# Pacing of interleaved work in a fused attention and FFN layer on eight cores

## What is computed

```python
def exterior(p1, p2):            # 6 components of p1 ^ p2, normalised
    parts = [p1[..., i] * p2[..., j] - p1[..., j] * p2[..., i] for i, j in _PAIRS]
    L = jnp.stack(parts, axis=-1)
    return L / jnp.maximum(jnp.linalg.norm(L, axis=-1, keepdims=True), 1e-12)

# attention: 16 heads, 6-component queries and keys, 64-wide values, causal
L_q = exterior((x @ W1_q.T).reshape(B, T, H, 4), (x @ W2_q.T).reshape(B, T, H, 4))
L_k = exterior((x @ W1_k.T).reshape(B, T, H, 4), (x @ W2_k.T).reshape(B, T, H, 4))
scores = jnp.einsum('bqhc,bkhc->bhqk', L_q, L_k @ _J6.T) * _SCALE
attn = jax.nn.softmax(jnp.where(causal, scores, -jnp.inf), axis=-1)
out = jnp.einsum('bhqk,bkhd->bqhd', attn, v) @ W_out.T + b_out
# FFN: W_real, W_imag are 512 x 512 each, unfolded from two small tensors
out_real = x_real @ W_real.T - x_imag @ W_imag.T + bias_real
out_imag = x_real @ W_imag.T + x_imag @ W_real.T + bias_imag
# layer: x + attention(xn) + ffn(xn)
```

## Time and profile before

| | us |
|---|---|
| median of 2 runs | 4972.77 (4968.52 and 4977.02) |
| the profiled execution | 4981.22 |
| its span, first to last instruction, slowest core (core 1) | 4980.2 |
| spans of all eight cores | 4961.6 to 4980.2 |
| busy: PE / DVE / ACT | 3447.8 / 1556.4 / 1477.3 |
| mean granted TensorE clock, cores 0 to 3 / 4 to 7 (median core) | 0.642 / 0.648 |

### The profile page before, as it was taken

The page is one execution under the profiler, slowest core; times in us unless marked ns, Lnnn a source line. Parts: engine busy times, 40 slices in busy tenths (PEclk is TensorE's granted clock), DMA queues, the critical chain, the costliest instruction groups (busy, mean ns, idle before and its releaser), DMA issues.

```text
span 4980.2 us, 37630 instructions; the slowest of 8 cores (4961.6 to 4980.2 us)
## 1 busy us (share of the span) xinstructions
PE 3447.8 (69%) x11040; PEld 1078.4 (22%) x11040; DVE 1556.4 (31%) x3089; ACT 1477.3 (30%) x1729; POOL 130.9 (3%) x197
## 2 busy tenths in 40 slices
PE   1137666777766866677766876677776787777776
PEld 0113211221111521222111432222111241111112
DVE  0543344432222334433122325533122222212211
ACT  0000033334422113333523203333433203454440
POOL 3000000000000000000000010000000000000001
PEclk9977855675555865576555775577555675555557
DMA  7100311120000131121000041112000021000004
GB/s 77 51 22 1 112 45 31 49 75 27 1 0 0 19 62 30 41 69 51 0 0 0 1 68 34 34 60 71 0 0 0 1 44 25 1 0 0 0 1 68
DMA packets 78284, 146.27 MB, mean 29 GB/s; under 512 B 39680, under 2 KB 42888, under 8 KB 78096
## 3 DMA queue, kind: packets, MB, share of 16 engines
q0 software_dynamic: 56000, 73.28, 7.8%
q1 hardware_dynamic: 22096, 70.59, 5.1%
HBM read 80.80 MB, written 69.21 MB: 30 GB/s over the span
## 4 chain that ended last, share of the span: by engine, by line
PE 53%; DVE 18%; DMA 10%; ACT 9%; issue 8%; DVEq 1%; POOL 0%; ACTq 0%; SPq 0%; POOLq 0%
PE O L546 16%; PE F L573 9%; PE S L506 8%; DMA y<-ost 7%; PE F L383 5%; DVE cdiv L579 3%; PE F L416 3%; DVE oT L587 3%; ACT exps L529 3%; ACT cdiv L566 2%; DMA xst<-x 2%; ACT cdiv L564 2%; PE F L423 2%; PE F L309 2%; DVE xnst L282 2%
## 5 line engine op out<-in xcount | busy, mean ns | idle before, releaser
L529 ACT ACTIVATE exps<-S 128x1024 bf16<-128x1024 f32 (+3 forms) x1280 | 1122.6, 893 | 2216.1 <-PE O L546 1559.1
L546 PE MATMUL O<-exps,vaug 128*65 128x512 bf16 (+3 forms) x2560 | 1075.4, 523 | 450.8 <-DVE oT L587 247.8
L506 PE MATMUL S<-fqp,fkp 6*128 6x512 bf16 x2560 | 709.2, 562 | 30.6 <-ACT exps L529 23.8
L573 PE MATMUL F<-cdiv,ones64f 1*64 1x512 f32 x512 | 461.0, 1051 | 206.1 <-ACT cdiv L566 201.0
L546 PEld LDWEIGHTS O<-exps,vaug 128*65 128x65 bf16 x2560 | 229.7, 138 | 982.9 <-issue 981.5
L579 DVE COPY cdiv<-F 64x512 f32<-64x512 f32 x256 | 164.0, 678 | 836.7 <-PE F L573 836.7
L537 DVE TENSOR_TENSOR exps<-exps,tri 128x256 bf16<-128x256 bf16 x512 | 142.7, 290 | 839.3 <-ACT exps L529 838.5
L295 PE MATMUL F<-idt,xnst 128*128 128x128 f32 x512 | 124.2, 424 | 351.9 <-DVE xnst L282 315.2
L506 PEld LDWEIGHTS S<-fqp,fkp 6*128 6x128 bf16 x2560 | 137.4, 98 | 881.4 <-issue 876.2
L456 PE MATMUL S<-wout,oT 128*128 128x512 bf16 x1024 | 271.3, 430 | 68.9 <-DVE ost L465 65.8
L383 PE MATMUL F<-wv,xnT 128*128 128x256 bf16 x2048 | 261.8, 291 | 3.3 <-DVE cdiv L579 3.1
(11 more groups left out here) (76 smaller groups left out, 2097.2 us busy)
## 6 DMA issues: line engine op xcount, KB each, us to landing
y<-ost POOLq DMA_DIRECT2D x128, 512.0 KB, 5.2
xst<-x SPq DMA_DIRECT2D x64, 512.0 KB, 3.6
xnst<-x SPq DMA_DIRECT2D x64, 512.0 KB, 4.3
wv<-wvT POOLq DMA_DIRECT2D x8, 256.0 KB, 18.1
wout<-woutT POOLq DMA_DIRECT2D x8, 256.0 KB, 18.6
tascr<-qk SPq DMA_DIRECT2D x16, 128.0 KB, 1.7
ost<-bout SPq DMA_DIRECT2D x1, 512.0 KB
ost<-bri SPq DMA_DIRECT2D x1, 512.0 KB
```

The source lines that it names most:

```text
L506: tS.inc(TE.matmul(S_ps[:, ss * 1024 + j * 512: ss * 1024 + j * 512 + 512], fk_pad[32 * m4:32 * m4 + 6, kt * 128:kt * 128 + 128], fq_pad[3 ...
L529: sS.inc(SE.activation(e_out, e_in, AF.Exp))
L546: ins = TE.matmul(O4[:, j * 512 + off:(j + 1) * 512], vaug[:, kt * 1040 + h * 65: kt * 1040 + h * 65 + 65], exp_sb[:, ss * 1024 + j * 512 ...
L573: tS.inc(TE.matmul(Fb[0:64, 0:512], ones64f_sb[:], cdiv[0:1, j * 512:j * 512 + 512], start=True, stop=True))
```

## The change

pace() no longer works at every fifth step but at every step, against a target that grows evenly over the 320 steps. The total is the sum of all weights, plus 4 for the V groups that are appended later. An item of weight 0 (A1) is charged 0.5 when it is taken, though it counts 0 in the total.

```diff
-            state = {"step": 0, "gate": False}
+            state = {"step": 0, "gate": False, "popped": 0.0}
+            total_items = sum(w for w, _ in q1) + sum(w for w, _ in q2) + (4 if b + 1 < nb else 0)
             def pace():
                 state["step"] += 1
-                if state["step"] % 5 == 0:
-                    wsum = 0
-                    while wsum < 1:
-                        if q1:
-                            w_, fn = q1.popleft()
-                        elif state["gate"] and q2:
-                            w_, fn = q2.popleft()
-                        else:
-                            break
-                        fn()
-                        wsum += w_
+                target = state["step"] * total_items / 320.0
+                while state["popped"] < target:
+                    if q1:
+                        w_, fn = q1.popleft()
+                    elif state["gate"] and q2:
+                        w_, fn = q2.popleft()
+                    else:
+                        break
+                    fn()
+                    state["popped"] += max(w_, 0.5)
```

## The result

The changed kernel takes 4949.94 us (median of 11 runs, 4942.92 to 4964.99) against 4981.15 before (10 runs): ratio 0.993, 95% interval 0.9911 to 0.995. When the forecast was made the kernel before had been timed only twice (4972.77).

What follows compares the result with a forecast made beforehand. The end is set by a chain of waits hopping between PE, ACT and DVE. Terms -5 + 16 + 9 + 2 = +22, taken as +20 a batch, +60 over three, gave 5041 profiled, 5033 us against the median; range 4975 to 5075.

Steps and rivals of the forecast that it cites:

- What bounds the kernel: Whole kernel: no engine full, a chain hops between PE, ACT and DVE; interleaved work adds to the path.
- Where the items go: In pace(): first queue ends at step 261, before 160; only 8 B items in the loop, the rest behind it.
- The tail and V: Behind the loop: last O to next first O grows from 122.2 to about 218 us; V itself +2 a batch.
- A: Normalising and transposing x tiles, split in two: sixteen tiles cost 84 us against 89.3, -5 us a batch.
- F: FFN passes, spread and moved: six at 6.9 us, ten at 3.0, 71 against 55, +16 us a batch.
- B in the loop: Eight B items in the loop cost 83 us; with four behind it 135 against 126.0, +9 us a batch.
- the signs that the prediction named: Changed profile: first to last O about 965 us, tail about 218, less transpose idle, FFN stage clock above 0.50.
- Rival 1: Interleaved items cost the same wherever they stand, only the order changes: 4973 to 4985 us; chance 0.14.
- Rival 2: First half of each A tile hides everywhere, three steps before the second: 4835 us, 2.8% faster; chance 0.04.
- Rival 3: FFN stage: clock stays at 0.50 through spread passes, 135 us a batch, 5225 us; chance 0.06, weaker forms included.
- Rival 4: Behind the loop: dense V groups are throttled, 9 us a batch more, 5060 us; chance 0.06.

Runs made afterwards that it cites:

- experiment 5: Changed kernel with only A's steps moved, first halves to 8, 19, 29, 36 of forty, second halves to 12, 24, 32, 40: 4796.9 us, ratio 0.9643.
- experiment 1: Changed kernel with B and V items put back at the steps of the kernel before: 4940.1 us, ratio 0.9907 to the kernel before.
- experiment 2: Changed kernel with A tiles and FFN passes put back at the steps of the kernel before: 4999.0 us, ratio 1.0038 to the kernel before.
- experiment 3: Changed kernel with the two halves of each A tile issued together again, at the second half's step: 5016.9 us, ratio 1.0074.
- experiment 6: Kernel of experiment 5 with the sixteen FFN passes of a batch all moved to ends of head pairs: 4709.9 us, ratio 0.9463.
- experiment 7: Changed kernel with DVE's square (L264) done twice: 5007.0 us, ratio 1.0055.
- experiment 8: Kernel of experiment 5 with all twelve B items in the loop and FFN passes at pair ends and unmasked steps: 4688.0 us, ratio 0.9418.
- experiment 9: Kernel of experiment 8 with four FFN passes and two B items moved to other steps: 4661.9 us, ratio 0.9358.
- experiment 4: Kernel before with only A split, first half three steps ahead of the second: 4985.3 us, ratio 1.001.

## Why the prediction was wrong, point by point

**What bounds the kernel.** Right for the places of both kernels: interleaved items are added to the path and not hidden, and each has a price of its place. It is no property of the items: at the places of experiment 5 sixteen tiles of A cost 12 to 18 us. Sums made in this way came within 1 to 8 us a batch in experiments 1, 2, 3, 5, 6, 7, 8 and 9; the one for experiment 4 (the split alone) missed by 19.

**Where the items go.** Right, by the windows.

**The tail and V.** Right: 95.7 us more were forecast behind the loop, 95 to 97 came. Experiment 2 isolates this half of the change and finds it a loss, as forecast.

**A, the step that failed first.** The forecast changed A by -5 us a batch, to 84, from four tiles at 20.9 us: 5.9, 8.0, 5.0 and 2.0. (Three slips of the working change nothing: 7.3 - 1.5 - 0.3 is 5.5 and not 5.6, the upper bound of F is 134 and not 135, and the window of 20.1 us holds steps 91 to 95 and not 90 to 95.) Steps 41 to 81 of batch 1, where the clock stayed low, have 4.9, 7.3, 4.8 and 1.9, which is 18.9 or 76 a batch. The timeline of the first place in the changed kernel:

```profile
650.34 1.22 DVE L264 TENSOR_TENSOR scr<-xst 128x1024 f32<-128x1024 f32 x1
...
654.76 0.29 ACT L275 ACTIVATE stat<-stat,cvec 128x1 f32<-128x1 f32 x1 [4.73 <-DVE stat L273]
...
655.34 1.28 ACT L529 ACTIVATE exps<-S 128x768 bf16<-128x768 f32 x2
655.75 1.23 DVE L282 TENSOR_SCALAR xnst<-xst,stat 128x1024 f32<-128x1024 f32 x1 [1.09 <-ACT stat L277]
...
656.28 0.61 PE L506 MATMUL S<-fqp,fkp 6*128 6x512 bf16 x2 [4.51 <-ACT exps L529]
656.83 0.46 DVE L537 TENSOR_TENSOR exps<-exps,tri 128x256 bf16<-128x256 bf16 x2
...
657.24 1.25 PE L546 MATMUL O<-exps,vaug 128*65 128x384 bf16 x4 [0.35 <-DVE exps L537]
...
659.31 1.94 PE L295 MATMUL F<-idt,xnst 128*128 128x128 f32 x8
...
662.30 3.64 PE L573 MATMUL F<-cdiv,ones64f 1*64 1x512 f32 x4
```

The mechanism of the wait is as forecast: the square starts at 650.34, right behind the mask, ACT waits 4.73 us at its Ln, PE waits 4.51 us for the exponential (656.28), the masks follow xnst (655.75, 656.83), and the transposes at 659.31 and the division behind them (662.30) stand without idle time. But the next O starts at 657.24, 6.9 us behind the square, and the row has four matmuls in 1.25 us: the pair behind it follows at once, its exponential having been done in the shadow of xnst. I had let only 0.3 us be caught up. By the ends of the O matmuls A1 at this place costs 5.0 us where I had 5.6, and at the second place 5.6 where I had 6.1. This part of the error is 84 - 76 = 8 us a batch.

The rest of A, 4 to 13 us a batch, is the clock, which the forecast left out of A's stage altogether, though it had counted it in F's. Windows of steps 15 to 21 and 55 to 61 of batch 1, the same code at the same place of forty, and the bare steps:

```profile
1852.00:1861.90 9.90, 8.81 (x37) 3.15 (x35) 2.41 (x4) 5.93 (x6) 0.00 (x0) 0.84 0.00 0
1957.40:1969.90 12.50, 12.48 (x37) 3.39 (x35) 3.24 (x5) 6.14 (x6) 0.00 (x0) 0.50 0.00 0
4146.10:4156.80 10.70, 10.70 (x30) 2.01 (x30) 0.58 (x2) 6.96 (x7) 0.00 (x0) 0.50 0.01 2
```

Granted 0.50 (second row), transposes and steps take 12.5 us; granted 0.84 they take 9.9, less than the bare 10.7. The same is seen over whole stages: of the 24 (eight cores, three batches) those granted 0.52 cost 70.4 and 72.0 us, those granted 0.55 cost 63.3 to 65.9, those granted 0.58 cost 59.2 to 60.1. Joined tiles hardly saw this (experiment 3: 0.50 to 0.52 over the stage); with the split PE reaches the transposes without a wait and stays busy through S, O and transposes, and in some tiles the clock then rises. That it does is shown; what decides in which tiles, no run settles. Nor is a higher clock enough by itself: the stages of experiment 4 were granted 0.54 to 0.57 and cost 90 to 93 us. My reading is that it pays where PE itself is on the path, as behind these transposes, and not where it waits for ACT and DVE. From 76 that leads to the 62 to 72 measured. Together A was mis-sized by 12 to 22 us a batch, 54 in all. This is most of the distance between forecast and result.

**F.** The direction was right and the size was not: 64 a batch instead of 71, against 55 before. In batch 1 the six passes ahead of a masked step cost 5.0 to 7.9 us, 6.5 on average against 6.9, and the ten others 0.9 to 4.9, 2.5 on average against 3.0. The cheaper ones tend to be those with a long unmasked stretch behind them; that more steps on the high clock pay for them is my reading, which no run isolates.

**B in the loop.** 74.5 instead of 83 in two of three batches. In batch 1 the three B1 cost 1.4, 2.1 and 3.0 instead of 3.5, three B2 12.3 to 13.2 (12.7 on average, where I had 14.0), and the two ahead of masked steps (281 and 301) 15.4 and 14.6, where I had 15.25.

So all three terms were on the dear side, and their errors added up: 3 x (84 - 66) + 3 x (71 - 64) + 3 x (83 - 77) = 93, about the 90 us between the 5041 forecast for the profiled execution and the 4951 measured. The rest is small and cancels: 4 us more in the tails, 6 by which the sum had been rounded down, 10 by which the later batches of the kernel before were dearer than batch 0. Of the signs that the prediction named, the stretch from a batch's first O to its last shrank to 929 to 937 us and not to 965; the others came as it said: the tail, the idle time before the transposes, and a clock above 0.50 in F's stage.

**Rivals.** Rival 1 (only the order changes) is refuted by experiments 1 and 2: the halves are worth -39 and +20 us. Rival 2 (A1 hides everywhere) is what happened at one place in four; experiment 7 shows that the other three lie on the path, and experiment 5 that places exist at which it is nearly true everywhere. Rival 3 (the clock stays low through F) did not happen: F's stage was granted 0.70. Rival 4 did not show on the core that sets the time: its four V groups in a row took 60.8 to 61.6 us, the tail being 218 as in the sum. But the slower V groups exist, and at about the size that was estimated (9 us). In the same execution cores 0 and 1 took 65 us for the third batch's V groups, at a granted clock of 0.88 and 0.89. In the profiled execution of experiment 3 cores 6 and 7, granted 0.79 to 0.81, took 68 to 69 us for those of the first two batches, with tails of 226 to 229 us; core 0, granted 0.97, took 60.8. A dense tail alone does not decide it, since most cores took 61 us for the same V groups.

## What to carry to other kernels

When work is interleaved by hand into in-order queues, its price is set by the place, not by the amount: a chain that crosses engines should start where the engine that begins it has run ahead, and a block of one engine should stand where that engine waits anyway. Here the even spread, which looks smoother, was worth 0.7%, and choosing the places by a table of prices read from the trace 6.4%. A run of the same loop without the interleaved work (here the last batch) gives a first table of prices; the price of a new place still has to be argued (the split alone was mispriced by 19 us a batch) and its terms should carry the clock of their stretch too, which here moved with the places.

## What the runs showed of the hardware

A stretch of one and the same code, 28 matmuls and 8 transposes, was granted 0.50 in one tile and 0.84 in another of the same batch, and took 12.5 or 9.9 us. Work added without a wait can then cost less than nothing: the stretch with the transposes was 0.8 us shorter than the one without them.

A higher granted clock did not always shorten a stage. In the changed kernel the stages of A cost 72.0 us at 0.52 and 59.2 at 0.58. In experiment 4 they were granted 0.54 to 0.57 and cost 90 to 93, no less than the 87 to 90 of the kernel before at 0.50 to 0.55, because PE's waits for the other engines grew as its busy time fell.

Beside 0.50 and 1.00 the records show a granted clock of 0.81, on one die at a time. In the profiled execution of the kernel before, core 1 was granted 0.81 from 2861 to 2934 us, while core 7 had 0.95 over the same stretch; in those of experiments 3, 5 and 8 it was the other die, and in those of 1, 2, 7 and 9 no core showed it. A comparison of the slowest cores of two executions can thus compare two dies.
